# One expert layer of a transformer stack: up projection computed transposed, down projection in three split passes

## The reference, cut to what matters

```
probs = softmax(x @ Wg.T); topk_vals, topk_idx = top_k(probs, 2); topk_vals /= sum(topk_vals)
combine[token, topk_idx] += topk_vals
for e in range(8):
    h = silu(x @ w1[e].T) * (x @ w3[e].T)        # 256 -> 704
    out = out + combine[:, e:e+1] * (h @ w2[e].T)  # 704 -> 256
```

## Time and profile before

| | us |
|---|---|
| median of three runs | 834.8 (828.1, 834.8, 835.23) |
| profiled execution, its own time | 828.73 |
| its span, first to last instruction | 826.9 |
| PE busy in the span | 755.4 (91%) |
| DVE, ACT, POOL busy | 519.9, 389.1, 306.7 |

### The profile page before, as it was taken

The page is one execution under the profiler, slowest core; times in us unless marked ns, Lnnn a source line. Parts: engine busy times, 40 slices in busy tenths (PEclk is TensorE's granted clock), DMA queues, the critical chain, the costliest instruction groups (busy, mean ns, idle before and its releaser), DMA issues.

```text
span 826.9 us, 15091 instructions
## 1 busy us (share of the span) xinstructions
PE 755.4 (91%) x5615; PEld 561.8 (68%) x5615; DVE 519.9 (63%) x843; ACT 389.1 (47%) x862; POOL 306.7 (37%) x348
## 2 busy tenths in 40 slices
PE   8889998899999899999987999988899889999994
PEld 6523334678888677868765899866788746676663
DVE  5998986688878757779886666546688441211110
ACT  2878888345544435434555666642455302112211
POOL 2178887414322234334680222321333221232221
PEclk8955555899999999999999999999799989999998
DMA  6199999212211213211220111110011449888842
GB/s 187 31 156 161 159 177 160 64 34 64 72 59 46 64 42 93 83 39 44 58 65 1 39 34 52 46 64 27 27 52 34 145 156 303 264 258 287 277 119 45
DMA packets 117446, 84.53 MB, mean 102 GB/s; under 512 B 79457, under 2 KB 100897, under 8 KB 117378
## 3 DMA queue, kind: packets, MB, share of 16 engines
q1 hardware_dynamic: 114498, 79.69, 35.9%
q0 software_dynamic: 2880, 3.93, 2.3%
HBM read 63.68 MB, written 3.67 MB: 81 GB/s over the span
## 4 chain that ended last, share of the span: by engine, by line
PE 59%; DVE 16%; POOL 9%; issue 6%; ACT 6%; DMA 3%; DVEq 0%; POOLq 0%; SPq 0%; ACTq 0%
PE ps L196 9%; PE ps L197 8%; PE ps L198 8%; PE ps L2417 7%; POOL pt L850 6%; PE ps L2437 4%; PE ps L1712 4%; PE ps L2093 2%; DVE x L1479 2%; PE ps L1182 2%; PE ps L1692 2%; DVE qrot L2265 2%; PE ps L2418 2%; POOL nb L857 2%; PE ps L2419 1%
## 5 line engine op out<-in xcount | busy, mean ns | idle before, releaser
L328 POOL TENSOR_TENSOR wa_lo<-raw,wa_hi 128x256 fp32r<-128x256 f32 (+1 forms) x76 | 86.2, 1139 | 183.2 <-ACT wa_hi L317 182.8
L328 POOL TENSOR_TENSOR wb_lo<-raw,wb_hi 128x256 fp32r<-128x256 f32 (+1 forms) x68 | 61.4, 907 | 131.6 <-ACT wb_hi L317 131.6
L953 ACT ACTIVATE kres<-ps,nb,qs 128x1024 int16<-128x1024 f32 x64 | 77.0, 1203 | 18.0 <-POOL nb L857 16.4
L1086 DVE TENSOR_REDUCE nm<-ps 128x1 f32<-128x1024 f32 x64 | 78.0, 1223 | 9.9 <-PE ps L776 7.5
L2613 DVE TENSOR_TENSOR hx<-act_g,ps 128x512 f32<-128x512 f32 x15 | 10.3, 688 | 105.1 <-ACT act_g L2497 105.1
L776 PE MATMUL ps<-qkt 48*128 48x512 bf16 x128 | 64.6, 606 | 6.3 <-ACT kres L953 4.7
L196 PE MATMUL ps<-xt_hi,wa_hi 128*128 128x512 f32 (+1 forms) x168 | 68.6, 409 | 1.6 <-DVE soft L1337 0.9
L850 POOL CAST pt<-pti 128x1024 bf16<-128x1024 int16 x62 | 64.2, 1036 | 6.7 <-DMA pti<-kres 3.3
L2417 PE MATMUL ps<-tw,xgt 128*128 128x512 f32 x120 | 64.5, 619 | 0.5 <-ACT xgt L2490 0.5
L197 PE MATMUL ps<-xt_lo,wa_hi 128*128 128x512 f32 (+1 forms) x168 | 64.9, 387 | 0.0
L198 PE MATMUL ps<-xt_hi,wa_lo 128*128 128x512 f32 (+1 forms) x168 | 64.7, 385 | 0.0
(11 more groups left out here) (407 smaller groups left out, 1944.1 us busy)
## 6 DMA issues: line engine op xcount, KB each, us to landing
tw<-w_l1f SPq DMA_DIRECT2D x15, 1920.0 KB, 8.6
raw<-w_l0a SPq DMA_DIRECT2D x16, 256.0 KB, 2.8
raw<-w_l1p SPq DMA_DIRECT2D x32, 128.0 KB, 2.1
raw<-w_l1x SPq DMA_DIRECT2D x32, 128.0 KB, 2.1
raw<-w_l1a SPq DMA_DIRECT2D x16, 256.0 KB, 2.7
raw<-w_l0f SPq DMA_DIRECT2D x12, 256.0 KB, 2.7
raw<-w_l0a SPq DMA_DIRECT2D x16, 128.0 KB, 2.1
wv_raw<-w_l0a SPq DMA_DIRECT2D x8, 256.0 KB, 3.1
```

The source lines that it names most:

```text
L328: last = nc.gpsimd.tensor_tensor(split_lo, src, split_hi.bitcast(F32), ALU.subtract)
L953: nc.scalar.activation(ei[:, n % RING, :], slot(n), ACT.Exp, bias=nb[:, n % 3:n % 3 + 1], scale=qs[:, col:col + 1], accum_out=sums[:, u, k ...
L1086: nc.vector.tensor_reduce(nm[:, n % 3:n % 3 + 1], slot(n), AX.X, ALU.max, negate=True).then_inc(x0["nm"], 1)
```

## The change

The operands of the up projection change places: the weights stand in the array (128 hidden rows at a time, 64 for the last chunk) and `xgt` streams, 128 columns. The product comes out transposed, hidden rows on the partitions, as the down projection wants it; `turn_h` and `h_copy` go. Gate and up take 768 columns each of the three banks of a tile. The down projection is made by `mm3`, three passes for each of six chunks; for it ACT copies `hx` to `hx_hi` and the down weights to `dw_hi`, and DVE subtracts to `hx_lo` and `dw_lo`. The load for tile m now waits for `up` and `dw_lo` of tile m - 4 in place of `down`. PE's order for m is `up(m)`, `gathered(m + 1)`, `down(m - 1)`; ACT's is `gate_of(m)`, `x_copy(m + 1)`, `h_high(m)`, `down_high(m + 1)`; DVE's is `product(m)`, `scaled(m - 1)`, `h_low(m)`, `down_low(m + 1)`. The gathered rows go to bank 6 and are copied by one instruction. Of the fillers, 8 after the weights of the slots become 12 before them, and 4 after the first gathered tile become 2. A memset of `hx` and its wait go.

```diff
-                    sp.wait_ge(mo["down"], mo_at("down", m - RAWS + 1))
+                    sp.wait_ge(mo["up"], mo_at("up", m - RAWS + 1))
+                    sp.wait_ge(mo["dw_lo"], mo_at("dw_lo", m - RAWS + 1))
...
+            busy(pe, 2, 12)
             pe.wait_ge(mo["weight_v"], mo_at("weight_v", 1))
...
-            busy(pe, 2, 8)
...
-                    last = nc.tensor.transpose(gathered_in_bank(c), xg[:, m % GATHERS, c * P:(c + 1) * P], ident[:])
+                    last = nc.tensor.transpose(ps[:, 6, c * P:(c + 1) * P], xg[:, m % GATHERS, c * P:(c + 1) * P], ident[:])
...
+            def up(m):
+
+                u, r = m % 2, m % RAWS
+                pe.wait_ge(mo["x_copied"], mo_at("x_copied", m + 1))
+                pe.wait_ge(tile_loaded[r], TURNED + 48 * (m // RAWS + 1))
+                if m >= 2:
+                    pe.wait_ge(mo["h"], mo_at("h", m - 1))
                 for g in range(2):
-                    cols = slice((2 * g + c) * P, (2 * g + c + 1) * P)
-                    nc.tensor.matmul(ps[:, b + 2 * g, :], xgt[:, u, c, :], tw[:, r, 0:4, cols], start=c == 0, stop=c == 1)
-                    nc.tensor.matmul(ps[:, b + 1, g * TAIL:g * TAIL + P], xgt[:, u, c, :], tw[:, r, 4, cols], start=c == 0 and g == 0, stop=False, skip_group_check=True)
-                    last = nc.tensor.matmul(ps[:, b + 1, g * TAIL + P:(g + 1) * TAIL], xgt[:, u, c, :], tw_part[:, r, 2 * g + c, :], start=False, stop=c == 1 and g == 1, skip_group_check=True)
...
+                    for k in range(FULL):
+                        for c in range(C2):
+                            nc.tensor.matmul(up_gate(m, g)[:, k * P:(k + 1) * P], tw[:, r, k, (2 * g + c) * P:(2 * g + c + 1) * P], xgt[:, u, c, :], start=c == 0, stop=c == 1)
+                    for c in range(C2):
+                        last = nc.tensor.matmul(up_gate(m, g)[0:PART1, FULL * P:WIDE], tw_part[:, r, 2 * g + c, :], xgt[:, u, c, :], start=c == 0, stop=c == 1)
+                last.then_inc(mo["up"], 1)
+
+            def down(m):
                 u = m % 2
-                pe.wait_ge(mo["h"], mo_at("h", m + 1))
+                pe.wait_ge(mo["dw_lo"], mo_at("dw_lo", m + 1))
+                pe.wait_ge(mo["h_lo"], mo_at("h_lo", m + 1))
                 if m:
-                    pe.wait_ge(mo["ht"], mo_at("ht", m))
                     pe.wait_ge(mo["scaled"], mo_at("scaled", m))
                 for k in range(FULL + 1):
-                    last = nc.tensor.transpose(turned_in_bank()[:, k * P:(k + 1) * P], hx[:, u, k * P:(k + 1) * P], ident[:])
-                last.then_inc(mo["h_t"], 1)
...
+                    rows = slice(0, P if k < FULL else PART1)
+                    cols = slice(k * P, (k + 1) * P)
+                    last = mm3(ps[:, 7, 0:D], (hx_hi[rows, u, cols], hx_lo[rows, u, cols]), (dw_hi[rows, u, k, :], dw_lo[rows, u, k, :]), k == 0, k == FULL)
+                last.then_inc(mo["down"], 1)
 
             gathered(0)
-            busy(pe, 2, 4)
+            busy(pe, 2, 2)
...
+            def h_high(m):
+                act.wait_ge(mo["h"], mo_at("h", m + 1))
                 if m >= 2:
                     act.wait_ge(mo["down"], mo_at("down", m - 1))
-                nc.scalar.activation(hxt[:, m % 2, :], turned_in_bank(), ACT.Copy).then_inc(mo["ht"], 1)
+                nc.scalar.activation(hx_hi[:, m % 2, :], hx[:], ACT.Copy).then_inc(mo["h_hi"], 1)
+
+            def down_high(m):
+                r, u = m % RAWS, m % 2
+                act.wait_ge(tile_loaded[r], TURNED + 48 * (m // RAWS + 1))
+                if m >= 2:
+                    act.wait_ge(mo["down"], mo_at("down", m - 1))
+                nc.scalar.activation(dw_hi[:, u, 0:FULL, :], tw[:, r, :, 4 * P:6 * P], ACT.Copy)
+                nc.scalar.activation(dw_hi[0:PART1, u, FULL, :], td_part[:, r, :], ACT.Copy).then_inc(mo["dw_hi"], 1)
...
+            def h_low(m):
+                dve.wait_ge(mo["h_hi"], mo_at("h_hi", m + 1))
+                nc.vector.tensor_tensor(hx_lo[:, m % 2, :], hx[:], hx_hi[:, m % 2, :].bitcast(F32), ALU.subtract).then_inc(mo["h_lo"], 1)
+
+            def down_low(m):
+                r, u = m % RAWS, m % 2
+                dve.wait_ge(mo["dw_hi"], mo_at("dw_hi", m + 1))
+                nc.vector.tensor_tensor(dw_lo[:, u, 0:FULL, :], tw[:, r, :, 4 * P:6 * P], dw_hi[:, u, 0:FULL, :].bitcast(F32), ALU.subtract)
+                nc.vector.tensor_tensor(dw_lo[0:PART1, u, FULL, :], td_part[:, r, :], dw_hi[0:PART1, u, FULL, :].bitcast(F32), ALU.subtract).then_inc(mo["dw_lo"], 1)
```

More of the change, by code:

```diff
@@ L110, in build @@
         xgt = sb("xgt", [P, 2, C2, P], ctx=mw)
-        act_g = sb("act_g", [P, 2, INTER], ctx=mw)
-        hx = sb("hx", [P, 2, (FULL + 1) * P], ctx=mw)
-        hxt = sb("hxt", [P, 2, (FULL + 1) * P], ctx=mw)
+        act_g = sb("act_g", [P, 2, WIDE], ctx=mw)
+        hx = sb("hx", [P, WIDE], ctx=mw)
+        hx_hi = sb("hx_hi", [P, 2, WIDE], F32R, mw)
+        hx_lo = sb("hx_lo", [P, 2, WIDE], F32R, mw)
         og = sb("og", [P, 2, D], ctx=mw)
@@ L177, in build @@
             "gather_at": ("k2", 2), "scatter_at": ("krep", 2), "x_t": ("idbf", 3), "x_copied": ("vti", 4),
-            "up": ("s", 64), "gate": ("nm", 64), "h": ("nb", 64), "h_t": ("e", 64), "ht": ("pt", 62),
-            "down": ("pv", 64), "scaled": ("rs", 8), "zeroed": ("y", 1), "count": ("at_t", 2), "table": ("at_hi", 2)}
+            "h_hi": ("vi", 2), "h_lo": ("vi_t", 2), "dw_hi": ("pta", 2), "dw_lo": ("out", 8), "up": ("s", 64), "gate": ("nm", 64), "h": ("nb", 64),
+            "down": ("pv", 64), "scaled": ("rs", 8), "count": ("at_t", 2), "table": ("at_hi", 2)}
         mo = {n: x0[first] for n, (first, _) in again.items()}
@@ L575, in build @@
         slot_w_lo = sb("slot_w_lo", [P, SLOTS], ctx=m5)
-        sb("spare_up", [P, 4 * INTER * 4 + 640], ctx=m5)
+        dw_hi = sb("dw_hi", [P, 2, FULL + 1, D], F32R, m5)
+        dw_lo = sb("dw_lo", [P, 2, FULL + 1, D], F32R, m5)
+        sb("spare_up", [P, 11904 - 4 * (FULL + 1) * D], ctx=m5)
         tw = sb("tw", [P, RAWS, FULL, 6 * P], ctx=m5)
@@ L2488, in x_copy @@
                     act.wait_ge(mo["up"], mo_at("up", m - 1))
-                for c in range(C2):
-                    last = nc.scalar.activation(xgt[:, m % 2, c, :], gathered_in_bank(c), ACT.Copy)
-                last.then_inc(mo["x_copied"], 1)
+                nc.scalar.activation(flat(xgt[:, m % 2, :, :]), ps[:, 6, 0:D], ACT.Copy).then_inc(mo["x_copied"], 1)
             def gate_of(m):
@@ L2496, in gate_of @@
                     act.wait_ge(mo["h"], mo_at("h", m - 1))
-                nc.scalar.activation(act_g[:, m % 2, :], up_gate(m), ACT.Silu).then_inc(mo["gate"], 1)
-            def h_copy(m):
-                act.wait_ge(mo["h_t"], mo_at("h_t", m + 1))
+                nc.scalar.activation(act_g[:, m % 2, :], up_gate(m, 0), ACT.Silu).then_inc(mo["gate"], 1)
+            def h_high(m):
+                act.wait_ge(mo["h"], mo_at("h", m + 1))
                 if m >= 2:
                     act.wait_ge(mo["down"], mo_at("down", m - 1))
-                nc.scalar.activation(hxt[:, m % 2, :], turned_in_bank(), ACT.Copy).then_inc(mo["ht"], 1)
+                nc.scalar.activation(hx_hi[:, m % 2, :], hx[:], ACT.Copy).then_inc(mo["h_hi"], 1)
[6 more added lines that the diff above has]
+                nc.scalar.activation(dw_hi[0:PART1, u, FULL, :], td_part[:, r, :], ACT.Copy).then_inc(mo["dw_hi"], 1)
             load_table(act, ACT.Silu)
+            down_high(0)
             for j in range(2):
@@ L2511, in l1f_act @@
             x_copy(0)
-            for m in range(TILES + 1):
-                if m:
-                    h_copy(m - 1)
+            for m in range(TILES):
+                gate_of(m)
                 if m + 1 < TILES:
                     x_copy(m + 1)
-                if m < TILES:
-                    gate_of(m)
+                h_high(m)
+                if m + 1 < TILES:
+                    down_high(m + 1)
         def l1f_dve(dve):
@@ L2608, in product @@
             def product(m):
-                u, b = m % 2, up_banks(m)
                 dve.wait_ge(mo["gate"], mo_at("gate", m + 1))
[L2611 to L2614, removed]
+                if m:
+                    dve.wait_ge(mo["h_lo"], mo_at("h_lo", m))
+                nc.vector.tensor_tensor(hx[:], act_g[:, m % 2, :], up_gate(m, 1), ALU.mult).then_inc(mo["h"], 1)
             def scaled(m):
@@ L2619, in scaled @@
                     dve.wait_ge(added, 16 * (m - 1))
-                nc.vector.tensor_scalar(og[:, m % 2, :], ps[:, 7, 2 * P:4 * P], slot_w[:, m:m + 1], None, ALU.mult).then_inc(mo["scaled"], 1)
+                nc.vector.tensor_scalar(og[:, m % 2, :], ps[:, 7, 0:D], slot_w[:, m:m + 1], None, ALU.mult).then_inc(mo["scaled"], 1)
             dve.wait_ge(mo["weights"], mo_at("weights", 1))
@@ L2626, in l1f_dve @@
             dve.wait_ge(step, c.up())
[L2627 to L2630, removed]
+            def h_low(m):
[6 more added lines that the diff above has]
```

(9 more changed lines are left out.)

29 lines of the change are left out of this document (4 added, 25 removed).

## The result

The changed kernel takes 824.2 us (median of 11 runs, 822.46 to 827.62), the kernel before 829.32 (median of 11, 827.65 to 835.23): a ratio of 0.9933, 95% interval 0.9911 to 0.9955. So it is faster by 0.7%. That is clear of no change, which the interval leaves out, and less than the 1% that I had set as the bound of no change. The forecast was 833, faster or slower by nothing that counts. It lies in the wide range, 820 to 841, only because that one reached down for rival 1, which did not happen: that is luck. The same runs also tell 0.7% from nothing, where the prediction held 1% to be the least that can be told.

A forecast was written before the change was run, and what follows sets the result against it. PE alone was taken to bound the tiles. Tiles -2.5, up(0) +0.8, clock +2.0, x_copy(1) +0.6 and end -1.3 sum to -0.4 us: 828.3 profiled, 834.4 on the median, forecast 833; own range 828 to 837, wide range 820 to 841.

The forecast's parts named there:

- rival 1: In the tile's up projection, the switch to 64-column weights costs nothing: 820 to 824 us; chance 0.27.
- the one on the dispatch: Before the tiles: moved fillers cost nothing, and the first gathered tile is still turned at 679.26, held by its gather.
- The clock: At up(0): PE idles 4 us just before, so the granted clock halves and up(0) loses 2.0 us (0 to 2.9).
- The tile: PE time per full tile: 8.79 us against 8.98, so -0.19 each and -2.5 over 13 tiles.
- the changes of shape: Switching the array's shape in a tile: 0.35 us for each of two 64-column groups, 0.38 for down's 64 rows.
- rival 2: In up, 64-column weights aren't loaded ahead within their group: slower by 9 us, 842 to 843; chance 0.10.
- Rival 3: In the tiles, scatters become the bound, beyond 10.5 us per scatter: 842 us; chance 0.04.
- What lies beside PE: ACT 3.9 and DVE 4.7 us per tile, loads, and scatters at 8.3 all stay within PE's tile time: no price.
- PE waits for `h_lo` at all: A sign, for the profile after, that would make the forecast wrong; cover of 4.5 us was expected before h_lo is late.
- `up(0)` and `x_copy(1)`: At the first tile: up(0) itself longer by 0.8 us, and x_copy(1) behind Silu, uncovered by a down projection, +0.6.
- The end: From the last up to the last scatter: 7.8 us instead of 9.1, so -1.3; the previous scatter lands in 3.7.
- The base: Starting time: runs at 828.1, 834.8 and 835.23, median 834.8; 833 was put since one run lay 7 us lower.

The follow-up runs named there:

- e1: The kernel before with only the fillers moved as in the change; ratio to before 0.9974, interval 0.9942 to 1.0006.
- e2: The changed kernel with the fillers put back where they were before; ratio to the kernel before 0.9938.
- e5: The changed kernel with six more fillers between the slot weights and the first gathered tile; ratio to the kernel before 0.9911.
- e4: e3 with the 64-row last chunk of down also run over all 128 rows, lower half zeros; 809.94 us, ratio to the kernel before 0.9765.
- e3: The changed kernel with the last chunk of up as 128-column instead of 64-column weights; 815.87 us, ratio to the kernel before 0.9803.
- e7: The changed kernel with the down projection left as two fp32 passes, no high and low parts; 834.03 us, ratio to the kernel before 1.0017.
- e8: e4 with the six added fillers of e5; 812.62 us, ratio to the kernel before 0.9777.

## Why the prediction was right or wrong

**The step that failed** is the one on the dispatch: "the first gathered tile is turned at 679.26 in any case (its gather takes that long, before the fillers end there as well)". It put an end that was set by PE down to a transfer. The row of the turn in the earlier trace rows has no bracket for a wait, the eight fillers stand directly ahead of it in the chain (676.02, 3.44 us), and the gather had landed about 2.6 us earlier if it took 4.9 as in after and `e1`; this trace doesn't have its landing, but the one of `e2`, with the same fillers, does, at 4.8. Moving the fillers brought `up(0)` forward by 3.2 us; I had booked nothing. Of these 3.2 the lower clock takes 1.7 back: net the moved fillers are worth 1.3 us in this kernel (`e2`) and 1.9 in the kernel before (`e1`). With this one term put right, my sum would have said -3.6 us, and 825.7 on the median of 11 runs.

**The clock** was right in mechanism and near in size: PE idle before `up(0)`, the granted clock at half in its first part, +1.7 us against +2.0; where fillers cover that time (`e2`, `e5`), `up(0)` runs at the full level. The size is in part luck: I had worked it out from a slow stretch of 5.8 us behind 4 us without work, and it was a shorter one behind 1.54 us. With the same fillers the first 20 passes lost 1.7 us in the changed kernel and in `e4`, but 0.8 in `e3` and `e7` (3.23 and 3.22), where the clock fell earlier. The slow stretch came one to two us earlier (677 to 681) than forecast, for the reason just given. With the wrong step the two fell apart: I booked the loss that the moved fillers bring and not the gain.

**The tile**: 8.70 against 8.79. Up takes 2 x (2.43 + 0.58) = 6.02 (6.03 forecast). The term that was mis-sized is that of the changes of shape. Against the 7.71 of passes alone, 0.99 us is left for three, where I had 2 x 0.35 + 0.38 = 1.08. `e3` shows 0.30 for each with 64 columns and `e4` 0.40 for the 64 rows. The reading from another stage (0.35) was 0.05 too high for columns. 0.09 x 13 = 1.2 us: the second largest part of the miss.

The Trainium skill's statement (TensorEngine Tiling (Array Packing), section Tiling Modes, Key Properties) that a change of tiling mode drains the engine agrees with `e3` and `e4`: both kinds of change cost, and both go when the shape stays, though no run shows that the loss is a drain.

**Rival 1** (a free change of columns) fell with `e3`; **rival 2** (64-column weights not loaded ahead) fell with the changed kernel itself, four passes in 0.58 with a change of shape in it and 0.45 in full width. The Trainium skill's sentence on weight loads (TensorE: Matmul & The Clock Gate, section The mechanism), taken at its word, is not borne out here: 48 passes with 48 weight loads stand 0.111 apart. **Rival 3** (scatters) had its condition for a moment and cost nothing: the first two scatters lay 10.37 us apart (695.21 to 705.58), four waited for a landing, 21.9 us of POOL's idle time, and PE never waited for them. At 8.1 and 7.7 us a tile (`e3`, `e4`) DVE waits for them, 2.2 and 5.1 us in all.

**What lies beside PE** cost nothing in the tiles, as forecast. "PE waits for `h_lo` at all" did happen, once and for 1.5 us: in the last down projection, which has no up projection ahead of it. By my own criterion that is a miss, and what it cost stands under the end, below.

**`up(0)` and `x_copy(1)`**: +0.87 and +0.40 against +0.8 and +0.6.

**The end**: -0.7 against -1.3. `down(13)` and its scatter came when forecast (2.5 and 3.3 us behind the last up), but that scatter landed 4.32 us later (808.14 to 812.46 in the chain), not the 3.7 that I took from the earlier trace rows. The last scatter follows 0.73 behind the landing, the handover that I had taken. The timeline shows that the engines were as late:

```profile
808.83 0.36 PE L197 MATMUL ps<-dw_hi,hx_hi 128*128 128x256 f32 x1 [1.49 <-DVE hx_lo L2617]
...
811.83 0.41 PE L199 MATMUL ps<-dw_hi,hx_lo 64*128 64x256 f32 x1
...
813.19 1.55 POOL L2452 DMA_INDIRECT sums_d<-og,scatter_idx  x1 [3.04 <-DVE og L2608]
```

PE waited 1.49 us for `hx_lo`, the granted clock fell to 0.57 in the microsecond from 810 and 0.50 in the next, and `down(14)` took from 808.83 to 812.24, 3.4 us instead of 2.3. DVE scaled until 812.76; with the 0.28 that lies between scaling and scatter elsewhere in this trace (738.43 to 738.71) the engines would have let the last scatter start at 813.04, the landing at 813.19. So the wait and the clock behind it are hidden by 0.15 us; I had the engines ready at 7.4 behind the last up and they were at 8.2. A faster scatter would bring little here.

**The sum**: 5.5 us between -0.4 and -5.9 are: dispatch 3.2, unchanged code ahead of it 0.9, the tiles 1.2, clock and start 0.4, after the last scatter 0.4, less 0.6 at the end. The first is the error. Why the last scatter's landing and the stores behind it took 0.4 less is open.

**The base**: I forecast 833 because one of three runs of before lay 7 us lower than the others. With 11 runs the median is 829.3, and the two high ones were at the edge. My sum on that base would have said 828.9.

## What to carry to other kernels

A last chunk that is half as wide or half as high is cheaper computed at full size, with its neighbour's columns or with zeros, than as a shape of its own: here three changes of shape cost 0.3 to 0.4 us each per tile, and removing them brought 1.7% on top of the change. Fillers that keep a clock up belong inside a wait that ends later than they do; to see whether they hold something, look whether the next instruction has a wait at all, and when its input had landed. And look at the clock behind the next wait as well: in `e8` it fell there instead. Where code ahead of the change varies from run to run by more than the effect, compare the traces from a mark behind it.

## What the runs showed of the hardware

- Passes that load a new 128 x 128 weight block each and stream 128 columns stand 0.111 us apart (`e4`: 20 in 2.23). Four passes with 64-column weights between them are no shorter and cost 0.30 us more for the change of shape (`e3`); three passes over 64 rows cost 0.40 more (`e4`).
- Much the same wait does not bring the low clock at the same moment, nor at the same price. PE was without work for 1.54 us in the changed kernel and 1.47 in `e3`; the granted clock fell 1.2 us after the end of that wait in the one (677.0) and before its end in the other (by 677.0, the wait ending at 677.35), and the first 20 passes took 4.13 and 3.23 us. It fell behind 1.85 us at `up(1)` of `e8` and not behind 1.41 in `e5`.
- The descriptors of a scatter took POOL 2.05 us in the changed kernel's tiles where they took 1.6 before, and 1.59 again in `e7`, which has no subtractions. In the changed kernel's timeline the subtraction runs when the scatter starts:

```profile
738.35 0.95 DVE L2617 TENSOR_TENSOR hx_lo<-hx,hx_hi 128x768 fp32r<-128x768 f32 x1
...
738.71 2.05 POOL L2452 DMA_INDIRECT sums_d<-og,scatter_idx  x1 [5.11 <-DVE og L2608]
```

  The lengthening agrees with the Trainium skill, page SBUF — State Buffer, section SBUF: two separate sides, by which a VectorE instruction with two inputs in SBUF and a GpSimd instruction that reads SBUF shut one another out. The other half does not show: DVE's subtractions took 0.95 and 1.49 us in every tile, with a scatter beside them or not, and the scatter at 730.56, which starts as `hx_lo` ends, took 1.59 though the next subtraction ran beside it from 730.91. It was off the path, and no run measured it by itself.
- The first gather landed 4.9 us after its issue in the changed kernel, 4.8 in `e1` and `e2`, 4.5 in `e5` and 5.1 in `e4`, though the loads of tile 1 are issued 0.8 us behind it; a scatter at the end, with no load running, took 4.3, and under the loads up to 10.37 lay from one to the next in the changed kernel and up to 10.08 in `e4`.
